# First attention of a fused audio tower: the product that makes the next group's tokens moved ahead of the turn of the local probabilities

## The reference

```
h = layer_norm(x, norm1_g, norm1_b)
q = h @ Wq.T
kv = h @ Wkv.T
...
lout = local_attn(head 0 of q, kv, kv)      # windows of 64, each looks at 3 windows
gout = linear_attn(heads 1..7 of q, kv, kv) # softmax of q and of k, k^T v, then q times it
attn = jnp.concatenate([lout, gout], axis=1)
y = attn.transpose(0, 2, 1, 3).reshape(b, n, c) @ Wproj.T + bproj
```

## Time and profile before

| | |
|---|---|
| three executions | 970.06, 970.06, 973.66 us; median 970.06 |
| the profiled execution | 971.51 us, span 969.7 us |
| PE busy | 918.6 us (95% of the span) |
| DVE, ACT, POOL busy | 704.9, 638.6, 518.5 us |
| mean granted clock of PE | 0.975 of full speed |
| the first attention | from about 153 to 260 us of the span |
| one round of it | 6.02 to 6.03 us |

### The profile page before, as it was taken

How to read it: one execution, slowest core, us unless ns; L and a number is a source line. 1 busy time by engine, 2 the same in 40 slices (tenths; PEclk the granted TensorE clock), 3 DMA queues, 4 the chain that set the end, 5 groups by cost and what they waited for, 6 DMA issues and landing times. The chain is left out here.

```text
span 969.7 us, 35416 instructions
## 1 busy us (share of the span) xinstructions
PE 918.6 (95%) x12660; PEld 668.5 (69%) x12660; DVE 704.9 (73%) x1984; ACT 638.6 (66%) x1214; POOL 518.5 (53%) x815
## 2 busy tenths in 40 slices
PE   8799987999798999999999998999999999979998
PEld 3355665777576888888888884666666666658887
DVE  4677657777666677878878778888888888975553
ACT  1355666888657577877778775777777777734444
POOL 0001016888583677787878876465555556462110
PEclk7899988999999999999999999999999999989999
DMA  6715000000000000000000000000000000000001
GB/s 131 197 34 130 1 1 1 2 0 0 2 1 1 3 3 2 0 0 0 0 0 0 1 3 1 2 2 0 0 0 0 0 0 0 2 2 19 22 22 28
DMA packets 10529, 14.82 MB, mean 15 GB/s; under 512 B 8832, under 2 KB 9088, under 8 KB 9536
## 3 DMA queue, kind: packets, MB, share of 16 engines
q1 hardware_dynamic: 10336, 13.56, 5.8%
q10 hardware_dynamic: 128, 0.39, 0.1%
HBM read 11.85 MB, written 2.10 MB: 14 GB/s over the span
## 5 line engine op out<-in xcount | busy, mean ns | idle before, releaser
L1892 ACT ACTIVATE e_hid<-ps,cst 128x512 f32<-128x512 f32 x256 | 155.0, 688 | 53.1 <-PE ps L1654 53.0
L1590 POOL TENSOR_TENSOR e_acc<-e_acc,e_part 128x512 f32<-128x512 f32 x96 | 122.2, 1273 | 34.6 <-DVE e_part L1820 27.7
L1666 PEld LDWEIGHTS ps<-ew,e_hid 128*64 128x64 f32 x4096 | 124.8, 138 | 21.9 <-issue 10.4
L1666 PE MATMUL ps<-ew,e_hid 128*64 128x64 f32 x4096 | 133.8, 224 | 0.0
L1654 PE MATMUL ps<-e_xs,ew 64*128 64x256 f32 x1024 | 128.1, 389 | 0.7 <-ACT e_hid L1892 0.7
L1820 DVE TENSOR_TENSOR e_part<-ps,e_wt 128x512 f32<-128x512 f32 x128 | 86.7, 687 | 44.9 <-PE ps L1666 41.6
L1654 PEld LDWEIGHTS ps<-e_xs,ew 64*128 64x128 f32 x1024 | 93.5, 186 | 16.2 <-issue 2.6
L2097 POOL TENSOR_TENSOR a_sum<-a_part 128x256 f32<-128x256 f32 x64 | 46.7, 729 | 90.0 <-DVE a_part L2207 90.0
L2167 PEld LDWEIGHTS ps<-cst,a_ex 128*128 128x128 f32 x512 | 55.8, 141 | 50.4 <-issue 50.4
L2196 DVE TENSOR_REDUCE a_rmax<-ps 128x8 f32<-128x1024 f32 x64 | 78.1, 1220 | 16.5 <-PE ps L2159 15.3
L2199 DVE TENSOR_TENSOR a_diff<-ps,a_rmax 128x1024 f32<-128x1024 f32 x64 | 78.3, 1224 | 2.9
(11 more groups left out here) (273 smaller groups left out, 1992.4 us busy)
## 6 DMA issues: line engine op xcount, KB each, us to landing
x_in<-x_dram SPq DMA_DIRECT2D x14, 384.0 KB, 6.1
cst<-cst_dram SPq DMA_DIRECT2D x1, 3101.0 KB, 15.3
out_dram<-e_res SPq DMA_DIRECT2D x16, 128.0 KB, 2.0
ew<-ew_dram SPq DMA_DIRECT2D x1, 1024.0 KB, 8.4
ew<-ew_dram SPq DMA_DIRECT2D x1, 512.0 KB, 9.3
cst<-cst_dram SPq DMA_DIRECT2D x1, 448.0 KB, 7.6
x_in<-x_dram ACTq DMA_DIRECT2D x2, 192.0 KB, 4.7
x_in<-x_dram SPq DMA_DIRECT2D x2, 192.0 KB, 5.3
```

The costliest lines, as they stand in the source:

```text
L1590: eng.tensor_tensor(acc[:, :, :, :], acc[:, :, :, :], part[n % RING][:, :, :, :], ALU.add).then_inc(sum_sb.sem, 1)
L1666: mm = eng.matmul(m.ps[rows, 6 + n % 2, to:to + C], hid[e % 8][:, a:a + C], w2[:, e * C:e * C + C], start=True, stop=True)
L1892: nc.scalar.activation(hid[e % 8][:, :].rearrange("p (r t) -> p r t", r=2), m.ps[:, 4 - 2 * (n % 2):6 - 2 * (n % 2), j * 256:(j + 1) * 256 ...
```

## The change

In PE's round the four products of `tokens` are issued behind `turn_queries` and ahead of `turn_probabilities`. Before, they stood behind `features`. Nothing is added or removed, and no other engine's order is touched.

```
             if back:
                 turn_keys(g - 1, 1 - b)
                 turn_queries(g - 1, g if left is not None else TG - 1)
+            if left:
+                tokens(g + 1, 1 - b)
+            if back:
                 turn_probabilities(g - 1)
                 context(g - 1, 1 - b)
             if left is None:
                 m.early["m0_turn"](eng)
             if left:
                 features(g + 1, 1 - b)
-                tokens(g + 1, 1 - b)
             if back:
                 attend(g - 1, 1 - b)
```

## The result

The changed kernel takes 982.69 us in the median of 17 executions (973.55 to 984.81), the kernel before beside it 970.51 us (969.11 to 982.06, 17 executions). The ratio is 1.0094 with a 95% interval of 1.0070 to 1.0117: slower by 0.9%. The medians are 12.2 us apart, the means 8.7 us (981.64 and 972.96), since the executions of the kernel before reach up to 982 us and most of the changed kernel's lie above 982. The forecast was 972.7 us, and 982.69 lies above its range. Timed again on another chip, the same kernel took 977.68 us against 972.03, ratio 1.0044 (1.0010 to 1.0078). Both numbers have to be explained.

What follows compares the result with a forecast made beforehand. The prediction took a 6.03 us ring of waits through PE, DVE and POOL as the bound, replaced by a longer one through ACT. Terms 1.35 + 0.91 + 0.5 - 0.2 = 2.6 us on 970.06 gave 972.7 us, range 971.0 to 975.1.

Steps and rivals of the forecast that it cites:

- the sum: Whole forecast over attention rounds 1 to 15: 1.35 + 0.91 + 0.5 - 0.2 = 2.6 us more.
- What bounds the kernel: First attention, before the change: waits from L1118 through L1073, DVE and POOL back to L1118 set each 6.03 us round.
- What takes its place: Attention rounds after the change: eight steps through ACT's copies, L1092 and L1073 give 6.16 us (odd) and 6.30 (even).
- DVE's wait ahead of the key maxima: Profile after, attention rounds: DVE loses its 0.64 us wait before L1186 and gets one of about that size before L1201.
- POOL's L984: Profile after, attention rounds: POOL finishes this instruction 0.1 to 0.6 us before L1118 asks for it.
- L1301 to L1092, 0.59 us: From the start of ACT's copy `q0T` to PE's local scores: 0.59 us, read where PE really waits for it.
- my 2.26: Extra time of the twelve later rounds: 1.35 us for five even ones plus 0.91 us for seven odd ones.
- Unknown costs: Possible deviations per round: PE's wait for ACT up to 0.09 us shorter, held-up issue up to 0.14 us longer; nothing taken.
- Going into round 2: nothing: Interval of L1118 into round 2: old 6.30 us, new 6.30 us, so no cost.
- Round 1, +0.5 us: L1118 of round 1 comes 0.46 to 1.05 us later, round 0 may give back about as much; 0.5 taken.
- Round 15, -0.2 us: Last interval, without product or turn of inputs: L1118 waits for POOL, as long as before or up to 0.3 us shorter.
- the rival of the falling clock: Chance 0.05: two short PE stalls per round lower the clock; 974.5 us for one fall, 992 or so if every round.

Runs made afterwards that it cites:

- kernel with only the surroundings changed: Against the kernel before, the product is moved in rounds 0, 1 and 14 alone, not in the loop's rounds: 973.60 us, ratio 0.9997.
- loop-only kernel: Against the kernel before, the product is moved in the loop's rounds 2 to 13 alone: 976.68 us against 972.14, ratio 1.0030.

## Why the prediction was wrong

The direction and the ring were right. Two steps failed: the sum took the stages behind the attention at the clock that they had before, and the way from L1301 to L1092 was taken as 0.59 us. The first put the time out of the range; the second made the rounds cost nearly twice what was forecast, which alone would have left about 975 us, inside it.

- **What bounds the kernel** (the ring through L1073, POOL and L1118): right. The kernel with only the surroundings changed shows it once more, at 6.02 and 6.03 us.
- **What takes its place** (the ring through ACT): right in every member. Seven of its eight steps came out within 0.02 us of the sum's. Two signs beside it were off: DVE's wait ahead of the key maxima was 0.28 us, not about 0.64, and POOL's L984 was done 0.88 us ahead of L1118, not 0.1 to 0.6.
- **L1301 to L1092, 0.59 us**: mis-sized, it was 0.74. The row is from round 0, where one semaphore instruction stands between ACT and the product; in the loop a register step follows it, which accounts for 0.09 us. Twelve rounds times 0.15 us are 1.8 of the 2.2 us by which the 4.5 us of these rounds exceed my 2.26. "Unknown costs" names about this size for a held-up issue, 0.14 us, but looks for it at L1073, where there was none, and then takes nothing.
- **Going into round 2: nothing**: wrong. It took 168.94 - 162.20 = 6.74 us, where the kernel before took 6.30. ACT needed 2.56 us from L1333 (162.86) to L1303 (165.42), not 2.22, as its exponentials waited for DVE's local maxima.
- **Round 1, +0.5 us**: from the first L1082 to L1118 of round 1 it is 10.46 us before, 10.28 in the first profile of the changed kernel, with the clock at 1.00 from 160 to 166 us, and 11.75 in the second, with the clock at 0.55 there. The term went with the clock, and the runs don't show what the order alone does.
- **Round 15, -0.2 us**: 251.52 - 245.78 = 5.74 against 6.03, -0.29.
- **The clock**: the rival of the falling clock looked for it inside the loop, with a chance of 0.05, and priced one fall at 1.8 us. It fell behind the loop, where PE waits several times in a row. From L1118 of round 15 to the MLP's first product it is 11.61 us before (248.30 to 259.91) and 14.14 after (251.52 to 265.66), 2.5 us more with the same instructions. The rival's sum for a fall in every round has a slip as well: twelve falls on top of the forecast make 994 us, not 992.
- **The sizes together.** 4.7 us for the rounds is shown on the timelines and, at equal clock, by the loop-only kernel (4.6) and the second run of the changed kernel (4.7). On the first chip the means are 8.7 us apart. The lower clock (0.9712 against the 0.975 of the profile before) accounts for 3.8 times 0.87 = 3.3 us by that kernel's own line; with the rounds that is 8.0, an estimate, as the clock of only one execution of the kernel before is on record there. The other 3.5 us of the 12.2 between the medians are the shape of the two scatters: the kernel before has its median 2.4 us below its mean, the changed kernel 1.1 above. Its mean, 972.96 us, is like those on the other chips (972.6 to 973.4). Why the changed kernel had a lower clock on the first chip and not on the other was not found.

## What to carry to other kernels

When an instruction is moved ahead of another to cut a ring of waits, write down the ring that the moved instruction's own inputs make and compare the two sums; here a stall of 0.2 us before a product made each round 0.3 to 0.45 us longer, because the product now stood ahead of the instruction that starts another engine's row of work. Take the time that an engine needs to wake behind another from the same kind of place, in or out of the loop, since a register step can stand between the wait and the instruction. Look at the timeline for where an added instruction really stands before reading its time: five fillers behind the wait that they were meant for test nothing. And where times scatter, compare means beside medians, and kernels at equal mean clock too: that told 4.7 us of work from the rest.

## What was unexpected of the hardware

Waits of PE of 0.4 to 1.5 us, one behind another, were enough for the clock to fall to 1.2 GHz, for 3 us and more in the kernel before and for more than 12 us in the changed one. A few dummy products among them (256 columns take 0.53 us, as from L1082 at 201.92 us to L1083 at 202.45) kept it at 2.4 GHz through 18 us, in both orders. A mean clock lower by 0.001 went with 0.5 to 1.1 us more in a kernel of 970 us. A register step between a wait and the product behind it cost 0.09 us each time that PE was waiting there.
